# Layer norm of x applied to its transpose, and two bias adds issued as accumulating transfers

## The chip, the core and the metric

The kernel runs on one core of a Trainium2 chip. The core has TensorE (PE, matrix products; its weight loads are listed as PEld), VectorE (DVE), ScalarE (ACT), GpSimd (POOL) and SyncE (SP), which here only issues transfers; transfers run on 16 DMA engines. SP's transfers are in the queue q1, those that GpSimd issues in q0. The engines run their own instruction streams and wait for each other by semaphores. The metric is device time of one execution in microseconds (us), median of several runs.

## The reference

One transformer layer over 32 batches of 224 rows of width 512, all in 32-bit floats, three residual blocks one after another:

```python
x = x + attn(layernorm(x))                      # 16 heads of 32, softmax over 224 keys, output weight Wff, bias bff
x = x + xattn(ctx, ctx, layernorm(x))           # one head of 512, 750 keys from ctx (32, 750, 512), bias bo
x = x + ffn(layernorm(x))                       # per row: top 8 of 2048 keys, softmax, sum of 8 rows of a value table, a gate
def layernorm(x): m = mean(x); v = var(x); return (x - m) / sqrt(v + 1e-5)      # over the 512 columns
# attn: q = n @ Wq.T / sqrt(512); k = n @ Wk.T; v = n @ Wv.T, n = layernorm(x)
```

## The kernel before

**Stages.** Each batch of 224 rows is held as two tiles of 112 rows (`T, R = 2, 112`). The work of a batch is cut into steps of four stages: A is the self-attention, X the cross-attention, F the router (top 8 search), G the weighted sum of the looked-up value rows. One iteration of the main loop works on batch i in A, i-1 in X, i-2 in F and i-3 in G, so that the four stages of four batches overlap. Iterations 0 to 2 and the last are written out, 3 to B-2 are a hardware loop (`Fori`). What is left of X, F and G after the last iteration, and the scaling and adding of the looked-up sums to the output (step Z), follow in the table `LAST`.

**Order.** The table `ORDER` lists the steps of an iteration. Each engine has a function for its part of a step, and `pipeline` (L286 ff.) calls them on every engine in the table's order. So each engine's stream is fixed, and an engine that waits holds back all that stands behind the wait. `SETUP` puts the one-time weight products (W) between the steps of iteration 0.

**PSUM.** A has four banks, X and F two each. `FILLS` says how many fills a step makes; they go round the banks, and a fill waits until the one before it in its bank is drained (`wait_free`, `wait_full`, `wait_drained`). The number of A's fills in an iteration must be a multiple of 4.

**The steps of A.** For batch b: `norm` (DVE, `a_norm`, L742) makes mean and 1/deviation of each row of `xa` and overwrites `xa` with (x - m) * rstd. `turn` transposes it on PE, 8 products with the unit matrix into two fills; ACT casts each fill to a rounded high part `xT[0]` (`turn_hi`, L567), DVE subtracts to get the low part `xT[1]` (`turn_lo`, L775). `qk` k (k = 0 to 3, four heads each) makes queries and keys, 24 products of 224 columns (three per pair: high-high, high-low, low-high); ACT casts the result (`qk_hi`), DVE makes the low part (`qk_lo`). `value` makes two fills of 12 products with 512 columns; ACT copies them to `va`. `score` k multiplies, `maxima` (L794) and the exponentials (L586) follow, `share` (L805, L807) divides by the sum, `prob` transposes the shares on PE (L994) and ACT copies them to `paT`, `mix` multiplies by the values (L1072), ACT copies to `oT`.

**The steps of X and F named below.** X `enter` is the product with Wff, to which DVE adds x with its bias (`x_enter`, L819, tile `xr`, result `x1`); X `norm` normalises `x1`; X `out` t is added to `x1` and gives `x2` (L844), freeing the two banks that `enter` needs. F `norm` normalises `x2` and takes the variance of the result, F `top` is the search (L861, L864).

**GpSimd.** `bias_x` (L502) adds the bias bff to `xr` once a batch, `bias_x1` (L509) adds `cb` to `x1`, `add_base` (L514) adds the normalised x2 to x2. In between GpSimd issues the look-ups, two indirect transfers for each of 8 chunks of a batch (L523), which G sums up (L888, L890) on DVE.

**Start.** SP issues some 20 loads of weights and small vectors, then `xr`; `split_hi` and `split_lo` (L658 ff., L905 ff.) cut Wq, Wk and Wv into a high and a low part, straight from the loaded tiles.

```python
("A", "norm", 0), ("X", "enter", 0), ("A", "turn", 0), ("G", "sum", 0), ("X", "norm", 0), ("A", "qk", 0),
("A", "value", 0), ("X", "turn", 0), ("G", "sum", 1), ("A", "score", 0), ("G", "sum", 2), ("X", "query", 0),
("A", "share", 0), ("F", "norm", 0), ("A", "prob", 0), ("A", "qk", 1), ("A", "qk", 2), ("G", "sum", 3),
```

## Time and profile before

| | |
|---|---|
| median of three runs | 2863.55 us (2862.77 to 2865.97) |
| the profiled execution's own time | 2859.07 us |
| its span, first to last instruction | 2857.2 us |
| busy: PE, PEld | 2649.0 us (93%), 1983.5 us (69%) |
| busy: DVE, ACT, POOL | 2104.9 us (74%), 1421.1 us (50%), 785.7 us (27%) |
| share of the chain that ended last | PE 90%, issue 2%, DVE 2%, DMA 2%, ACT 1%, POOL 1% |
| transfers | 313.05 MB; q1 19.2% and q0 17.4% of the 16 engines' span |

A row of the chain or of a timeline begins with its start in us and its length; `L985` is a line of the kernel, `psA<-xT_hi,wqT_hi` the tile written and those read, `x48` the number of instructions. Successive matrix products overlap in their rows, so the pace is read from start to start. The hardware loop's iterations are alike; that of the rows below begins near 1587 us.

### The profile page before, as it was taken

The numbers are of one execution on the slowest core, as the hardware profiler recorded it, in microseconds if no ns is written. First come the engines' busy times: TensorE is split into PE (matmuls) and PEld (weight loads), VectorE is DVE, ScalarE is ACT, GpSimd is POOL, SyncE is SP. The second block draws the span as 40 slices with busy tenths as digits, with TensorE's granted clock in tenths as the row PEclk, the third lists the DMA queues.
The fourth block names the chain that finished last, engine by engine and source line by source line (L and its number), as shares of the span: only waits on it lengthen the run. The fifth ranks groups of instructions, "written<-read, shape, count | busy, mean of one in ns | idle before, by whom it ended". The sixth has DMA issues, their size and how long they took to land.

```text
span 2857.2 us, 53958 instructions
## 1 busy us (share of the span) xinstructions
PE 2649.0 (93%) x18042; PEld 1983.5 (69%) x18042; DVE 2104.9 (74%) x4071; ACT 1421.1 (50%) x4214; POOL 785.7 (27%) x651
## 2 busy tenths in 40 slices
PE   6899999999999999999999999999999999999830
PEld 4667777777777777777777777777777777777610
DVE  4446778878777788877777878777788877777652
ACT  2345554445455444555554445455544455555343
POOL 0001323222223232222323222223232222233245
PEclk9999999999999999999999999999999999999965
DMA  5112323333333332333323333333332333333799
GB/s 167 57 57 76 103 91 118 103 102 105 107 101 100 102 120 86 108 107 109 103 91 116 110 96 104 107 101 104 99 120 89 107 107 110 101 93 108 180 237 181
DMA packets 102683, 313.05 MB, mean 110 GB/s; under 512 B 14577, under 2 KB 15089, under 8 KB 94417
## 3 DMA queue, kind: packets, MB, share of 16 engines
q1 hardware_dynamic: 54002, 180.37, 19.2%
q0 software_dynamic: 48640, 132.16, 17.4%
q8 instruction: 23, 0.38, 0.1%
q14 instruction: 18, 0.15, 0.0%
HBM read 269.35 MB, written 43.12 MB: 109 GB/s over the span
## 4 chain that ended last, share of the span: by engine, by line
PE 90%; issue 2%; DVE 2%; DMA 2%; ACT 1%; POOL 1%; SPq 1%; POOLq 0%; DVEq 0%; ACTq 0%
PE psX L985 45%; PE psA L985 19%; PE psF L985 8%; PE psA L994 8%; PE psA L1072 4%; PE psA L1049 4%; PE psX L994 3%; DMA vg<-in_L_ffn_aux_values,idx 1%; DVE xT_lo L775 1%; PE psF L994 1%; ACT xT_hi L567 1%; POOL out L540 1%; POOL vg L523 0%; SPq L371 0%; ACT paT L550 0%
## 5 line engine op out<-in xcount | busy, mean ns | idle before, releaser
L523 POOL DMA_INDIRECT vg<-in_L_ffn_aux_values,idx x512 | 516.5, 1009 | 1635.1 <-DVE agg L890 830.9
L586 ACT ACTIVATE pa<-psA,nmax 112x224 f32<-112x224 f32 x1024 | 443.6, 449 | 150.3 <-DVE nmax L794 147.6
L890 DVE SCALAR_TENSOR_TENSOR agg<-vg,wt,agg 112x512 f32<-112x512 f32 x420 | 367.5, 875 | 16.2 <-DMA vg<-in_L_ffn_aux_values,idx 2.9
L794 DVE TENSOR_REDUCE nmax<-psA 112x4 f32<-112x896 f32 x256 | 266.7, 1083 | 149.8 <-PE psA L1049 149.8
L985 PE MATMUL psX<-big,gT 128*112 128x375 f32 x1024 | 333.4, 478 | 1.3 <-ACT nx L622 1.0
L985 PE MATMUL psX<-pT,cx 125*128 125x224 f32 x1536 | 307.5, 357 | 0.0
L550 ACT COPY paT<-psA 112x448 f32<-112x448 f32 x512 | 236.5, 544 | 111.1 <-PE psA L994 108.7
L985 PEld LDWEIGHTS psX<-pT,cx 125*128 125x128 f32 x1536 | 285.5, 190 | 7.7 <-issue 0.3
L807 DVE TENSOR_TENSOR pa<-pa,rsum 112x896 f32<-112x896 f32 x256 | 279.5, 1092 | 8.8
L985 PEld LDWEIGHTS psX<-big,gT 128*112 128x112 f32 x1024 | 177.4, 176 | 127.1 <-ACT nx L622 1.2
L985 PE MATMUL psX<-m,xnxT 128*112 128x512 f32 x512 | 235.6, 603 | 0.0
L994 PEld LDWEIGHTS psA<-ident,pa 112*112 112x112 f32 x2048 | 206.3, 136 | 42.3 <-issue 22.3
L994 PE MATMUL psA<-ident,pa 112*112 112x112 f32 x2048 | 227.6, 263 | 5.5 <-DVE pa L807 5.5
L985 PE MATMUL psX<-wffT,oT 128*112 128x512 f32 x512 | 225.0, 592 | 0.6 <-ACT oT L550 0.6
L586 ACT ACTIVATION_READ_ACCUMULATOR pa<-psA,nmax 112x1 f32 x1024 | 212.4, 207 | 0.0
L985 PE MATMUL psX<-xnxT,m 128*128 128x224 f32 x1024 | 204.5, 358 | 0.6 <-ACT xnxT L550 0.6
L572 ACT CAST qk_hi<-psA 128x448 fp32r<-128x448 f32 x128 | 68.2, 532 | 267.0 <-PE psA L985 267.0
L985 PE MATMUL psA<-xT_hi,wqT_hi 128*128 128x224 f32 x512 | 155.7, 304 | 46.9 <-DVE xT_lo L775 46.9
L985 PEld LDWEIGHTS psX<-xnxT,m 128*128 128x128 f32 x1024 | 192.9, 192 | 6.0 <-ACT xnxT L550 4.5
L985 PEld LDWEIGHTS psX<-wffT,oT 128*112 128x112 f32 x512 | 88.5, 177 | 131.7 <-issue 130.6
L861 DVE MAX8 top<-sc 112x8 f32<-112x2048 f32 x64 | 146.5, 2289 | 38.0 <-ACT sc L550 38.0
L622 ACT ACTIVATE nx<-psX,xmax 112x375 f32<-112x375 f32 x128 | 72.2, 569 | 203.4 <-DVE xmax L825 203.4
(195 smaller groups left out, 5301.5 us busy)
## 6 DMA issues: line engine op xcount, KB each, us to landing
big<-in_ctx_t SPq DMA_DIRECT2D x32, 1500.0 KB, 6.7
cx<-in_ctx SPq DMA_DIRECT2D x32, 1500.0 KB
xa<-in_x SPq DMA_DIRECT2D x32, 448.0 KB, 4.7
xr<-in_x SPq DMA_DIRECT2D x32, 448.0 KB, 3.9
out<-x SPq DMA_DIRECT2D x32, 448.0 KB, 3.1
agg_scratch<-agg SPq DMA_DIRECT2D x60, 224.0 KB, 6.4
vg<-in_L_ffn_aux_values,idx POOLq DMA_INDIRECT x512, 3.7
over_weights<-agg_scratch SPq DMA_DIRECT2D x15, 448.0 KB, 13.5
```

Of the source, the lines that this page charges most:

```text
L523: pool.indirect_dma_start(vg[:, c % SLOTS, k, :], None, aux_values, bass.IndirectOffsetOnAxis(ap=idx[:, t, n:n + 1], axis=0))\
L550: nc.scalar.copy(dst, src).then_inc(drained[s][j % banks[s]], 1)
L586: last = nc.scalar.activation(pa[:, t, h, :], psA[0:R, h, t * S:(t + 1) * S], ACT.Exp, bias=nmax[:, k % 2, h, t:t + 1], accum_out=rsum[:, ...
L622: nc.scalar.activation(px[:, t, j * HK:(j + 1) * HK], bank("X", job)[0:R, 0:HK], ACT.Exp, bias=xmax[:, t:t + 1], accum_out=xsum[:, t, j:j ...
L794: nc.vector.tensor_reduce(nmax[:, k % 2, h:h + 2, :], psA[0:R, h:h + 2, 0:T * S].rearrange("p h (t s) -> p h t s", t=T), AX_X, ALU.max, ne ...
L807: nc.vector.tensor_tensor(pa[:, t, :, :], pa[:, t, :, :], rsum[:, k, t, :].unsqueeze(2).to_broadcast([R, HB, S]), ALU.mult).then_inc(a_sha ...
L861: mark("F", nc.vector.max(top[:, t, :], sc[0:R, :]))
L890: last = nc.vector.scalar_tensor_tensor(dst, vg[:, c % SLOTS, k, :], w, dst, ALU.mult, ALU.add)
L985: last = nc.tensor.matmul(dst, stationary, moving, start=n == 0, stop=n == len(pairs) - 1)
L994: return nc.tensor.transpose(dst, src, ident[0:k, 0:k])
L1049: last = nc.tensor.matmul(psA[0:R, h, t * S:(t + 1) * S], qkT[q][own, k % 2, t * R:(t + 1) * R], qkT[key][own, k % 2, S:2 * S], start=n == ...
L1072: last = nc.tensor.matmul(bank("A", j)[h * DH:(h + 1) * DH, 0:S], va[:, c, HB * k + h, :], paT[:, c, h, :], start=c == 0, stop=c == T - 1)
```

## The change

**x turned outside.** A new input `x_t` holds x of each batch already transposed. SP loads it to `centered` (128 x 896). PE's `turn` of A is gone, and with it the normalisation of `xa`: DVE only takes the row statistics (stage N, for the batch after the one in A; 13 short steps). SP stores 1/deviation of the 224 rows to DRAM and loads them back spread over 128 partitions (`spread`). DVE multiplies `centered` by it, ACT casts to `xT[0]`, DVE subtracts for `xT[1]` (step N `center`).

**No mean in x.** The mean is taken out of the weights instead: at the start PE makes the column mean of Wq, Wk, Wv (a product with a matrix of 1/512), and DVE subtracts it from each before the split.

**value in quarters.** Four fills of 256 columns take the place of two of 512, so 48 products instead of 24; ACT copies four times.

**Biases.** `bias_x` and `bias_x1` are transfers that GpSimd issues with an accumulating add, 448 KB each, from the bias tile in SBUF.

**Order.** `ORDER` is a new table, `FIRST` stands before iteration 0, and the iteration before the last is written out too. `LAST` is unchanged.

```diff
-    ("A", "norm", 0), ("X", "enter", 0), ("A", "turn", 0), ("G", "sum", 0), ("X", "norm", 0), ("A", "qk", 0),
...
+    ("X", "enter", 0), ("X", "norm", 0), ("A", "qk", 0), ("G", "sum", 0), ("A", "value", 0), ("X", "turn", 0),
...
+    ("A", "prob", 3), ("F", "score", 3), ("A", "mix", 3), ("N", "center", 0), ("X", "out", 1), ("F", "top", 1),
-FILLS = {("A", "turn"): 2, ("A", "qk"): 1, ("A", "value"): 2, ("A", "score"): HB, ("A", "prob"): 2 * T,
+FILLS = {("A", "qk"): 1, ("A", "value"): 2 * T, ("A", "score"): HB, ("A", "prob"): 2 * T,
+FIRST = (("W", "mean", 0), ("N", "norm", 0), ("N", "spread", 0), ("W", "split", 0), ("W", "mean", 1), ("N", "center", 0),
+         ("W", "split", 1), ("W", "mean", 2), ("W", "split", 2),
+         ("W", "keys", 0), ("W", "keys", 1), ("W", "keys", 2), ("W", "keys", 3))
...
-                batch = {"A": i, "X": i - 1, "F": i - 2, "G": i - 3, "W": 0}
+                batch = {"N": i + 1, "A": i, "X": i - 1, "F": i - 2, "G": i - 3, "W": 0}
...
-            sp.dma_start(xa[:, :, :], tiles(row(x, 0))).then_inc(x_loaded, 16)
+            sp.dma_start(xa[:, :, :], pairs(row(x, 0))).then_inc(x_loaded, 16)
+            sp.dma_start(flat(centered), row(x_t, 0)).then_inc(xt_loaded, 16)
...
+            def store_moments(b, _):
+                sp.wait_ge(steps["N"], N_STEPS * (b + 1))
+                sp.dma_start(row(moments_dram, b), rstd["N"][:, :]).then_inc(moments_stored, 16)
+                if not (isinstance(b, int) and b == B - 1):
+                    sp.dma_start(xa[:, :, :], pairs(row(x, b + 1))).then_inc(x_loaded, 16)
+
+            def spread_moments(b, _):
+                sp.wait_ge(moments_stored, 16 * (b + 1))
+                wait(sp, xt_scaled, b)
+                sp.dma_start(spread[:, :], row(moments_dram, b).rearrange("r t -> (r t)").partition_broadcast(P))\
+                    .then_inc(moments_spread, 16)
+
+            def next_xt(b, _):
...
+                sp.wait_ge(xT_split, b + 1)
+                sp.dma_start(flat(centered), row(x_t, b + 1)).then_inc(xt_loaded, 16)
...
-                    nc.gpsimd.tensor_tensor(xr[:, :, :], xr[:, :, :], bff[:, :].unsqueeze(1).to_broadcast([R, T, D]),
-                                            ALU.add).then_inc(xr_biased, 1)
+                    apart(pool)
+                    pool.dma_start(xr[:, :, :], bff[:, :].unsqueeze(1).to_broadcast([R, T, D]), accum_op=ALU.add)\
+                        .then_inc(xr_biased, 16)
...
-                nc.gpsimd.tensor_tensor(x1[:, :, :], x1[:, :, :], cb[:, :].unsqueeze(1).to_broadcast([R, T, D]),
-                                        ALU.add).then_inc(x1_biased, 1)
+                apart(pool)
+                pool.dma_start(x1[:, :, :], cb[:, :].unsqueeze(1).to_broadcast([R, T, D]), accum_op=ALU.add)\
+                    .then_inc(x1_biased, 16)
...
+            def center_hi(b, _):
+
+                act.wait_ge(xt_scaled, b + 1)
+                wait_full(act, "A", max(FILL["A", "value", 0] + 2 * T - 1, FILL["A", "qk", NB - 1]), b - 1)
+                nc.scalar.copy(xT[0][:, :, :], centered[:, :, :]).then_inc(xT_hi, 1)
...
+            def scaled_x(b):
+                dve.wait_ge(xt_loaded, 16 * (b + 1))
+                dve.wait_ge(moments_spread, 16 * (b + 1))
+                nc.vector.tensor_tensor(centered[:, :, :], centered[:, :, :], spread[:, :].unsqueeze(1).to_broadcast([P, C, S]),
+                                        ALU.mult).then_inc(xt_scaled, 1)
+
+            def center_lo(b, _):
+                scaled_x(b)
+                dve.wait_ge(xT_hi, b + 1)
+                lo(xT[1][:, :, :], centered[:, :, :], xT[0][:, :, :]).then_inc(xT_split, 1)
...
+            def split_lo(_, n):
+                w = (wqT, wkT, wvT)[n]
+                nc.vector.tensor_tensor(staged[n], staged[n], made_next().unsqueeze(1).to_broadcast([P, C, D]), ALU.subtract)\
+                    .then_inc(setup_drained, 1)
...
-                    wait_drained(pe, "A", FILL["A", "turn", 0] + 1, b)
+                    pe.wait_ge(xT_split, b + 1)
...
+                for t in range(T):
+                    for half in range(2):
+                        j, cols = FILL["A", "value", 0] + 2 * t + half, slice(half * D // 2, (half + 1) * D // 2)
+                        wait_free(pe, "A", j, b)
...
+            def mean_weight(_, n):
+                if n == 0:
+                    pe.wait_ge(const_ready, 2)
+                pe.wait_ge(weight_loaded[n], 16)
+                product(place(), [(over_d, staged[n][:, c, :]) for c in range(C)]).then_inc(setup_full, 1)
```

`place()` waits until the setup product three before it is drained, so the fourth product of the router's keys (fill 6) waits for the third subtraction.

On PE, at the seam of the hardware loop and the first steps behind it, the kernel before (`wffT,oT` is X enter, `ident,xa` the transposes, `xT,wqT` the first of qk 0):

```order
L252 REGISTER_ALU
L985 MATMUL psX<-wffT,oT 112x512 x8
L1017 REGISTER_ALU
L252 REGISTER_ALU
L994 MATMUL psA<-ident,xa 128x112 x8
L252 REGISTER_ALU
L985 MATMUL psA<-xT_hi,wqT_hi 128x224
```

and the changed one:

```order
L257 REGISTER_ALU
L1041 MATMUL psX<-wffT,oT 112x512 x8
L1079 REGISTER_ALU
L257 REGISTER_ALU
L1041 MATMUL psA<-xT_hi,wqT_hi 128x224
```

The eight transposes are gone, and qk 0 follows X enter directly.

On DVE, at the start, the kernel before, behind the norm of batch 0 (`wqT_lo`, `wkT_lo`, `wvT_lo` are the split of the weights, `wffT<-psX` the router's keys):

```order
L738 TENSOR_SCALAR xa<-xa,mv_A,rstd_A 112x512 x2
L909 SCALAR_TENSOR_TENSOR wqT_lo<-cx,wqT_hi 128x512 x4
L909 SCALAR_TENSOR_TENSOR wkT_lo<-m,wkT_hi 128x512 x4
L909 SCALAR_TENSOR_TENSOR wvT_lo<-m,wvT_hi 128x512 x4
L913 COPY xnxT<-bvc 128x4x112
L775 TENSOR_TENSOR xT_lo<-psA,xT_hi 128x448 x2
L916 TENSOR_SCALAR wffT<-psX 112x512 x2
```

and the changed one, behind the statistics of batch 0 (`cx<-cx,psX` and `m<-m,psX` take the mean out of Wq and Wk, `m<-m,psF` out of Wv):

```order
L959 TENSOR_TENSOR cx<-cx,psX 128x2048
L964 SCALAR_TENSOR_TENSOR wqT_lo<-cx,wqT_hi 128x512
L964 SCALAR_TENSOR_TENSOR wqT_lo<-cx,wqT_hi 128x512 x3
L827 TENSOR_TENSOR centered<-centered,spread 128x896
L822 TENSOR_TENSOR xT_lo<-centered,xT_hi 128x896
L959 TENSOR_TENSOR m<-m,psX 128x2048
L964 SCALAR_TENSOR_TENSOR wkT_lo<-m,wkT_hi 128x512
L964 SCALAR_TENSOR_TENSOR wkT_lo<-m,wkT_hi 128x512 x3
L959 TENSOR_TENSOR m<-m,psF 128x2048
L964 SCALAR_TENSOR_TENSOR wvT_lo<-m,wvT_hi 128x512
```

The split of Wk and Wv now stands behind the multiplication by `spread`, which waits for the round through DRAM.

On DVE, at share 0 (`rsum` and `pa`), the kernel before (`stats_F` begins F norm):

```order
L883 ISA
L890 SCALAR_TENSOR_TENSOR agg<-vg,wt,agg 112x512
L709 REGISTER_ALU
L890 SCALAR_TENSOR_TENSOR agg<-vg,wt,agg 112x512
L805 RECIPROCAL rsum<-rsum 112x4
L709 REGISTER_ALU
L807 TENSOR_TENSOR pa<-pa,rsum 112x896
L805 RECIPROCAL rsum<-rsum 112x4
L709 REGISTER_ALU
L807 TENSOR_TENSOR pa<-pa,rsum 112x896
L252 REGISTER_ALU
L716 BN_STATS stats_F<-x 112x6 x2
```

and the changed one (`mv_F` and `var_all` are the end of F norm, `qk_lo` the low part of qk 1):

```order
L815 BN_AGGR mv_F<-stats_F 112x2 x2
L749 REGISTER_ALU
L818 ISA
L818 COPY var_all<-mv_F 112x2
L857 RECIPROCAL rsum<-rsum 112x4
L749 ISA
L859 TENSOR_TENSOR pa<-pa,rsum 112x896
L857 RECIPROCAL rsum<-rsum 112x4
L749 REGISTER_ALU
L859 TENSOR_TENSOR pa<-pa,rsum 112x896
L837 REGISTER_ALU
L822 TENSOR_TENSOR qk_lo<-psA,qk_hi 128x448
```

F norm now stands between the maxima of score 0 and share 0. On PE, prob 0 has moved from ahead of qk 1 and qk 2 to behind them and F turn.

## Rows read from the trace of the kernel before

**Rows 1.** Busy time by stretch: us, each engine's busy time (instructions), PEclk, DMA share, GB/s

```profile
357.00:2500.00 2143.00, 2105.88 (x14567) 1585.58 (x14566) 1693.49 (x3281) 1110.07 (x3354) 606.84 (x493) 1.00 0.33 104
```

**Rows 2.** The chain that ended last, whole run: start us, us, what

```profile
26.29 8.49 PE psA L985 x48
...
122.89 8.52 PE psA L985 x48
...
2588.16 8.52 PE psA L985 x48
```

**Rows 3.** The same chain, in one iteration

```profile
1587.26 10.48 PE psX L985 x24
1597.74 0.47 PE psA L994 x4
...
1598.24 0.54 ACT xT_hi L567
...
1599.34 0.62 DVE xT_lo L775
...
1600.01 8.52 PE psA L985 x48
...
1616.40 1.53 PE psA L994 x16
```

**Rows 4.** Waits: who for whom, us in total, times, longest

```profile
PE psA L985 <- DVE xT_lo L775: 46.9, 32, 2.7
```

**Rows 5.** Timeline of PE in that iteration: start us, us, instruction

```profile
1600.22 0.27 PE L985 MATMUL psA<-xT_lo,wqT_hi 128*128 128x224 f32 x1
...
1602.79 0.39 PE L985 MATMUL psA<-wvT_hi,xT_hi 128*112 128x512 f32 x1
...
1608.37 0.93 PE L994 MATMUL psX<-ident,nx 112*128 112x112 f32 x8
```

**Rows 6.** Timeline of DVE in that iteration

```profile
1601.72 1.28 DVE L716 BATCH_NORM_STATS2 stats_X<-x 112x6 f32<-112x512 f32 x2
...
1607.12 3.37 DVE L890 SCALAR_TENSOR_TENSOR agg<-vg,wt,agg 112x512 f32<-112x512 f32 x2
1610.40 2.08 DVE L794 TENSOR_REDUCE nmax<-psA 112x4 f32<-112x896 f32 x2
1612.40 1.53 DVE L890 SCALAR_TENSOR_TENSOR agg<-vg,wt,agg 112x512 f32<-112x512 f32 x2
...
1616.55 1.28 DVE L716 BATCH_NORM_STATS2 stats_F<-x 112x6 f32<-112x512 f32 x2
...
1623.86 1.14 DVE L775 TENSOR_TENSOR qk_lo<-psA,qk_hi 128x448 fp32r<-128x448 f32 x2
```

**Rows 7.** Timeline of POOL in that iteration

```profile
1606.74 2.40 POOL L509 TENSOR_TENSOR x<-x,cb 112x1024 f32<-112x1024 f32 x1 [1.96 <-DVE nx L738]
...
1621.52 2.38 POOL L514 TENSOR_TENSOR x<-x,nx 112x1024 f32<-112x1024 f32 x1 [4.09 <-DVE nx L738]
```

**Rows 8.** Transfers by line: number, KB each, median us from issue to landing

```profile
agg_scratch<-agg SPq DMA_DIRECT2D x60, 224.0 KB, 6.4
...
out<-over_weights POOLq DMA_DIRECT2D x15, 448.0 KB, 13.5
```

**Rows 9.** Timelines of PE and DVE at the start

```profile
18.01 3.72 PE L985 MATMUL psX<-sc,gT 128*112 128x512 f32 x4 [3.19 <-DMA unc1T<-in_L_ffn_unc_w]
...
52.31 2.28 DVE L775 TENSOR_TENSOR rkL<-wffT,rkS 49x2048 fp32r<-49x2048 f32 x1
```

**Rows 10.** The chain at the start

```profile
19.45 4.96 DMA gbc<-in_L_ffn_gate_bias
...
46.98 3.45 PE psX L985 x8
...
59.10 5.61 PE psA L985 x48
...
66.18 0.88 PE psA L1049 x23
```

More of the change, by code:

```diff
@@ L302, in iteration @@
                         step[s, name](b, arg)
+            for s, name, arg in FIRST:
+                if (s, name) in step:
+                    step[s, name](0, arg)
             for i in range(3):
                 iteration(i)
-            with eng.Fori(3, B - 1) as i:
+            with eng.Fori(3, B - 2) as i:
                 iteration(i)
+            iteration(B - 2)
             iteration(B - 1)
@@ L478, in _ @@
                           ("W", "cb"): first_cxT, ("W", "gb"): first_ctx,
-                          ("X", "score"): next_cxT, ("X", "mix"): next_ctx, ("A", "turn"): next_x, ("X", "enter"): next_xr,
+                          ("X", "score"): next_cxT, ("X", "mix"): next_ctx, ("N", "norm"): store_moments,
+                          ("N", "spread"): spread_moments, ("N", "center"): next_xt, ("X", "enter"): next_xr,
                           ("F", "norm"): store_base,
@@ L798, in share @@
             def share(b, k):
+                if k == 0:
+                    count["A"] = 0
                 for t in range(T):
@@ L971, in _ @@
                            ("W", "gb"): made_gb,
-                           ("A", "norm"): a_norm, ("A", "turn"): turn_lo, ("A", "qk"): qk,
+                           ("N", "norm"): x_moments, ("N", "center"): center_lo, ("A", "qk"): qk,
                            ("A", "score"): maxima, ("A", "share"): share,
@@ L1033, in value @@
                     pe.wait_ge(split, 3 * C)
-                wait_drained(pe, "A", FILL["A", "turn", 0] + 1, b)
+                pe.wait_ge(xT_split, b + 1)
                 for t in range(T):
-                    j = FILL["A", "value", 0] + t
-                    wait_free(pe, "A", j, b)
-                    filled("A", j, product3(bank("A", j)[0:R, :], [(both(xT, ALL, c, slice(t * R, (t + 1) * R)),
-                                                                    both(wvT, ALL, c, ALL)) for c in range(C)]))
+                    for half in range(2):
+                        j, cols = FILL["A", "value", 0] + 2 * t + half, slice(half * D // 2, (half + 1) * D // 2)
+                        wait_free(pe, "A", j, b)
+                        filled("A", j, product3(bank("A", j)[0:R, 0:D // 2],
+                                                [(both(xT, ALL, c, slice(t * R, (t + 1) * R)), both(wvT, ALL, c, cols))
+                                                 for c in range(C)]))
             def scores(b, k):
```

142 lines of the change are left out of this document (76 added, 66 removed), and 23 rows, old and new, of tables (ORDER, SETUP).

## The prediction

> **What bounds the kernel now.** I read the views in this order. The table of busy time by stretch shows the steady part: PE is busy 2105.88 of 2143 us, 98%, at the full clock (granted 1.00, so 2.4 GHz), DVE 79%, ACT 52%, the DMA engines 33% [rows 1]. So there a microsecond counts only if it is PE's. The chain of waits confirms it: it runs through PE, and one batch's qk 0 follows the last at a fixed distance. From the one at 1600.01 to that of batch 31 at 2588.16 are 12 batches, 82.35 us each [rows 2, 3]. Inside an iteration the chain leaves PE at one place only: after X enter come the transposes of `xa` at 1597.74, then ACT's cast, DVE's subtraction, and PE goes on at 1600.01, 2.27 us later [rows 3]. The list of waits has the same hole, 46.9 us in 32 waits, 1.47 us each [rows 4]; the rest of the 2.27 us is the transposes. Everything else in the iteration is PE work end to end.
>
> **Part 1, the transposes and their wait: -2.27 us a batch.** X enter is now followed by qk 0, which waits for `xT_split`. Is that in time? N center stands on DVE behind the last G sum and on ACT behind the copy of mix 3. From mix 3 on, PE has X out 1 and X enter to do, 10.48 us [rows 3]. In that time ACT must copy mix 3 (about 0.3) and cast 896 columns: 448 took 0.54, so 1.08 [rows 3]. DVE must subtract 896 columns: share 0, two reciprocals and two products of that size, takes 2.6 us in all (from the end of the 1.53 us sum at 1612.40 to F norm at 1616.55), so at most 1.3 [rows 6]. Together 2.7 us, and X out's second half, which DVE now takes behind it, is only full after 3.6 us. The 1/deviation is made early: N norm stands behind G sum 1, some 25 us after qk 0, and center at about 68. Within these 40 us lie a store and a load through DRAM; the nearest rows are 6.4 us for a store of 224 KB and 4.96 us for a small load in the crowded start [rows 8, 10]. So nothing is late next here.
>
> **Part 2, value in quarters: +0.43 us a batch.** The trace has no product of 256 columns of this kind. From 1600.22 to 1602.79 are 23 products of 224 columns, 0.1117 us each; from 1602.79 to 1608.37 24 of 512, 0.2325 us each [rows 5]. Between them a column costs 0.00042 us, so 256 columns cost 0.125 us and 48 products 6.01 us, against 5.58 now. Bounds: 48 times 0.1117 is 5.36 (a gain of 0.22), 48 times 0.2325 is 11.16 (a loss of 5.58). I take the line, since 224 columns lie next to 256 and have weight loads at least as wide (128 columns against 112).
>
> The Trainium skill (TensorE: Matmul & The Clock Gate, Back-to-back issue gap) says that the spacing of products is set by the weight load and the product together; the change doubles value's weight loads. Were the loads the bound, value would go to 11.16 us, and the whole to 2818 + 30 x 5.15 = 2972. The 0.1117 us of qk, with 24 loads of 128 columns, speaks against it: this trace has the load hidden. I give that under 1 in 100.
>
> **Part 3, the biases: 0 on PE.** GpSimd loses two adds of 2.4 us an iteration [rows 7] and gets two issues of 448 KB. No accumulating transfer into SBUF is in the trace. The nearest row, an accumulating transfer of 448 KB to DRAM in the crowded end, lands after 13.5 us [rows 8]; I take that as the upper bound and nothing as the lower. What covers it: `x1` is biased behind X norm and used in X out over 50 us later, `xr` at mix 0 and used in X enter 35 us later. Behind the bias of `x1` in GpSimd's queue stand the look-ups of chunk 2; they are summed in G sum 2, and between G sum 0 and G sum 2 DVE has maxima (2.0), F norm (7.3), share 0 (2.6) and more [rows 6], over 20 us. If the cover went, DVE would wait for the look-ups, and PE behind it.
>
> What goes besides is a stall of DVE: two sums of G took 3.37 us beside GpSimd's add to `x1`, two like them 1.53 us right after [rows 6, 7]. These 1.84 us are DVE's, in a stretch where PE does not wait for it, so they count nothing.
>
> The Trainium skill (SBUF — State Buffer, Who interferes with whom) has the rule for it: a DVE instruction with two SBUF inputs and a GpSimd instruction that reads SBUF exclude each other for a whole instruction. The trace agrees with the 3.37 against 1.53. The rule also speaks against the new order, see the first rival.
>
> **Part 4, the start: +9.5 us up to the second qk 0.** Before, the first qk 0 is at 26.29 [rows 2]. Now it waits for a round through DRAM. SP comes to the store of the deviations behind its twenty-odd loads: the last small one was issued at 19.45, `xr` comes 0.5 later, and the new load of `x_t` lies ahead of them (up to 1.6), so 22.0. The store lands as the small load did, 4.96 us later, 27.0; the load back, with little beside it, 4.0 later (my choice below those 4.96 us), 31.0 [rows 10]. Then multiply, cast, subtract: 1.2 + 1.1 + 1.2, 34.5. Only then does DVE come to Wk: a subtraction of 2048 elements, 2.28 us [rows 9], four casts (0.54 times 512/448, 0.62 each) and the last low part, 0.7: 40.0. Then the subtraction for Wv, 42.3, which the router's fourth key product waits for; two instructions at 0.93 us (four such took 3.72 when PE had just been idle [rows 9]): 44.2. So qk 0 comes 17.9 us late. Iteration 0 gives some back: before, PE was done with m2 at 50.43 and waited for share 0, and did qk 1 and qk 2 from 59.10 on, so that score 1 came at 66.18 [rows 10]. Now qk 1 and qk 2 stand in that wait, and score 1 follows prob 0 and its last copy, at 59.7: -6.5. With +0.4 for value and -2.3 for the transposes the second qk 0 moves from 122.89 by +9.5. Bounds: the round in half the time is 4.5 us less; both transfers as slow as 13.5 us is 18 more.
>
> **The sum.** +9.5 up to batch 1's qk 0, then 30 batches at -2.27 + 0.43 = -1.84 are -55.2, and value of batch 31 +0.4. The tail (`LAST`) is the same work. Together -45.3. The profiled execution took 2859.07 us (span 2857.2 and 1.9 around it), so 2813.8; the median of the runs lies 4.5 above that execution, so 2818.
>
> **Rivals.**
>
> First, slower: F norm now stands ahead of share 0, and prob 0 waits for share 0 and for the low parts of qk 1 and qk 2 (its last fill needs qk 2's bank). Counted from qk 0, DVE's maxima begin 2.03 us after X turn [rows 5, 6], which stands at 2.78 + 6.01 = 8.79: 10.8. With 2.0, F norm 7.3, share 0 2.6 and the two low parts 1.1, DVE is done at 23.9. PE reached prob 0 8.0 us after X turn [rows 3, 5]; with qk 1 and qk 2 (5.4) and F turn (0.9) it is there at 23.1, at its last fill at 24.2. The slack is 0.3 us. GpSimd's add of F starts when DVE's normalised x2 is there and runs 2.38 us [rows 7]; before, what came behind F norm at 1623.86 met its end at 1623.90. If the add comes late, because GpSimd is still issuing, it would hold share 0, which reads two SBUF tiles, for up to 2.38 us: 2.1 us a batch, 63 in all, 2881. It decides from a delay of 0.3 + 1.84 us. Against it: GpSimd has nothing to issue just then, G sum 0's look-ups being done about 5 us before.
>
> Second, a smaller gain: on ACT the two copies of F score 0 now stand directly ahead of the four of prob 2, and score 3 needs the banks that these free. Two copies of 512 columns are 1.2 us; if all of it falls on PE, 37 us, 2855, if half, 2837. For it: PE has only F score 1 between prob 2 and score 3, about 0.9 us. Against it: the copies of prob 2 are not longer than before, and ACT has been idle for part of F score 0's time.
>
> Third, the change does not do what it says: qk 0 waits for `xT_split` as it did for `xT_lo`, 1.47 us a batch, 2862. The slack worked out in part 1 speaks against it.
>
> **Numbers.** Forecast 0.70, its own range 2800 to 2836 (value between its lower bound and the line, the start between -5 and +18). Second rival 0.16, 2836 to 2862. Third 0.05. First 0.09, 2860 to 2881 and beyond. What a measurement of this kernel can tell from no change is about 0.2%, 5.7 us: faster is below 2857.8. That is the forecast and most of the second rival, 0.84; the third and the rest of the second, 0.06; slower 0.10. The range 2799 to 2855 leaves out the first and the third rival and the end of the second.
>
> **What would show it.** Right: 80.5 us from qk 0 to qk 0, 12 products of 256 columns in 1.50 us, no wait of PE between X enter and qk 0, the first qk 0 near 44 us and the second near 132. Wrong: a row in the list of waits of PE on `pa` or `qk_lo` of 30 or so times near 1 us (first rival), on `paT` (second) or on `xT_lo` (third); waits of DVE on the look-ups, which would mean that the accumulating transfers hold GpSimd's queue; a low granted clock in the steady part.

## The result, and the profile after

The changed kernel takes 2846.36 us (median of five runs, 2843.18 to 2849.35) against 2862.77 us of the kernel before, run on the same chip: 0.9941 of its time, 95% interval 0.9928 to 0.9953, so 16.4 us faster. The forecast was 2818. The profiled execution has a span of 2841.4 us where the kernel before had 2857.2: 15.8 us less, and these are accounted for below.

First the start. The chain of waits of the changed kernel, with the columns start, length, what:

```profile
21.43 6.17 DMA moments_scratch<-rstd_N
...
27.62 4.29 DMA spread<-moments_scratch
...
32.00 1.10 DVE centered L827
...
37.42 0.64 ACT wkT_hi L702
...
38.15 2.50 DVE wkT_lo L964 x4
...
42.90 2.05 PE psF L1041 x2
44.95 5.09 PE psA L1041 x36
...
132.23 8.23 PE psA L1041 x72
...
207.44 8.24 PE psA L1041 x72
287.34 8.23 PE psA L1041 x72
...
2571.39 8.23 PE psA L1041 x72
```

The round through DRAM, Wk behind it, the third subtraction and the router's last key product come one after the other as the prediction had them; the first qk 0 is at 44.95 us and the second at 132.23, 9.3 us later than before [rows 2]. From there to the qk 0 of batch 31 at 2571.39 are 30 batches and 2439.16 us; before they took 2465.27 [rows 2]. That is 26.1 us less, where the prediction has 55.2. The tail, 270.0 us against 269.0, adds 1.0. Together +9.3 - 26.1 + 1.0 = -15.8.

So the miss is in the 30 batches. The row 207.44 to 287.34 shows that not all of them are alike: iteration 2 takes 79.90 us, less than the 80.5 predicted. It has no batch in stage G yet, but that alone is not it: in the kernel before the same iteration takes 82.31 us (200.27 to 282.58), as much as those of its loop. From 287.34 on, 28 batches take 81.57 us each. The changed kernel's busy time over the stretch of [rows 1]:

```profile
357.00:2500.00 2143.00, 2105.62 (x15125) 1625.67 (x15124) 1677.70 (x3256) 1129.41 (x3394) 544.08 (x499) 1.00 0.47 123
```

PE is still at 98% and at the full clock. What is left of its waits, from 380 to 2570 us (engine, line, whom it waits for, us in total, times, longest):

```profile
PE psA L1130 <- ACT pa L626: 30.6, 27, 1.2
PE psA L1050 <- DVE qk_lo L822: 6.5, 25, 0.7
```

The wait for `xT_lo` [rows 4] is gone. Two others have come: mix 2 (L1130) waits for ACT's exponentials, 1.13 us in each of 27 batches, and prob 0 (L1050) for the low part of a qk, 0.26 us in each of 25 by this list. The list counts idle time only. By the starts, more is lost: X score, which follows prob 0, comes 0.4 us later after qk 0 in the iteration at 1591.86 than in iteration 2, and X out 0, which stands behind mix 2 and F score 2, 1.6 us later. Mix 2 puts its result into a bank that holds score 3 until the exponentials have read it. Here is the timeline of PE from the last products of score 3 to mix 2 and F score 2 (the idle time before an instruction and its releaser stand in brackets):

```profile
1647.83 0.30 PE L1107 MATMUL psA<-qk_hi,qk_lo 32*112 32x224 f32 x4
1648.06 4.81 PE L1041 MATMUL psX<-pT,cx 125*128 125x224 f32 x24
1654.01 0.96 PE L1130 MATMUL psA<-paT,va 112*32 112x224 f32 x16 [1.15 <-ACT pa L626]
1654.90 0.48 PE L1041 MATMUL psF<-rkS,rqS 112*112 112x512 f32 x1
```

DVE's maxima of score 3, ACT's last exponentials, and GpSimd's look-ups at the same time:

```profile
1649.49 2.09 DVE L844 TENSOR_REDUCE nmax<-psA 112x4 f32<-112x896 f32 x2 [2.08 <-PE psA L1107]
```

```profile
1650.62 0.45 ACT L626 ACTIVATE pa<-psA,nmax 112x224 f32<-112x224 f32 x1 [2.50 <-DVE nmax L844]
...
1653.74 0.46 ACT L626 ACTIVATE pa<-psA,nmax 112x224 f32<-112x224 f32 x1
```

```profile
1646.56 0.93 POOL L562 DMA_INDIRECT vg<-in_L_ffn_aux_values,idx  x1 [9.99 <-DVE agg L942]
1647.79 0.92 POOL L562 DMA_INDIRECT vg<-in_L_ffn_aux_values,idx  x1 [0.30 <-issue]
```

The same place in the kernel before, on PE and DVE:

```profile
1655.78 0.28 PE L1049 MATMUL psA<-qk_hi,qk_lo 32*112 32x224 f32 x4
...
1660.48 0.55 PE L985 MATMUL psF<-rkS,rqS 112*112 112x512 f32 x1
...
1661.65 0.96 PE L1072 MATMUL psA<-paT,va 112*32 112x224 f32 x16
```

```profile
1656.18 2.09 DVE L794 TENSOR_REDUCE nmax<-psA 112x4 f32<-112x896 f32 x2 [2.97 <-PE psA L1049]
```

Two things are to be seen. The row behind mix 2 is F score 2: in the kernel before it stood ahead of mix 2, and the new order has it behind, so only X mix 1 (4.81 us) lies between score 3 and mix 2. And the last product of score 3 ends at 1647.83 + 0.30 = 1648.13, but DVE, idle and waiting for PE, starts at 1649.49, 1.36 us later. Iteration 2, where GpSimd issues nothing between 228 and 271 us, has the same two instructions on PE and DVE like this:

```profile
263.03 0.29 PE L1107 MATMUL psA<-qk_hi,qk_lo 32*112 32x224 f32 x4
263.26 4.81 PE L1041 MATMUL psX<-pT,cx 125*128 125x224 f32 x24
267.99 0.96 PE L1130 MATMUL psA<-paT,va 112*32 112x224 f32 x16
```

```profile
263.43 2.09 DVE L844 TENSOR_REDUCE nmax<-psA 112x4 f32<-112x896 f32 x2 [3.63 <-PE psA L1107]
```

There DVE starts 0.11 us after the product's end, and mix 2 follows X mix 1 without a wait. The first profile of the kernel before has 0.12 at this place. The Trainium skill (TensorE: Matmul & The Clock Gate, The cost: per-tile semaphore tail) says that the semaphore increments of several tiles' products come one after another; for four tiles with four increments, as in a score, its formula gives 0.15 us, an estimate. The 0.11 us measured here lies near that, and the 1.36 us is not explained by it.

The same stands at score 0, whose end falls on the look-ups of G sum 0, here on PE, DVE and POOL:

```profile
1601.40 0.28 PE L1107 MATMUL psA<-qk_hi,qk_lo 32*112 32x224 f32 x4
...
1614.99 1.04 PE L1050 MATMUL psA<-ident,pa 112*112 112x112 f32 x8 [0.16 <-DVE qk_lo L822]
```

```profile
1602.50 2.09 DVE L844 TENSOR_REDUCE nmax<-psA 112x4 f32<-112x896 f32 x2 [2.32 <-PE psA L1107]
```

```profile
1601.04 1.01 POOL L562 DMA_INDIRECT vg<-in_L_ffn_aux_values,idx  x1 [1.45 <-DVE agg L942]
```

The maxima start 0.82 us after the product's end (1601.68), where iteration 2 has 0.11, and F norm, share 0 and the low parts of qk 1 and qk 2, which stand behind them on DVE, come that much later for prob 0.

### The profile page after: what moved, and what is told of

The parts are those of the page before. It is cut to its first block, busy times and chain, and to the rows that moved or that the text cites. A ratio compares the mean times of both kernels' runs of the same rounds, so it can differ in the third digit from the quotient of the medians.

```text
span 2841.4 us, 55248 instructions
## 1 busy us (share of the span) xinstructions
PE 2633.9 (93%) x18578; PEld 2016.2 (71%) x18578; DVE 2075.9 (73%) x4010; ACT 1436.4 (51%) x4246; POOL 702.9 (25%) x652
## 4 chain that ended last, share of the span: by engine, by line
PE 74%; DVE 10%; issue 8%; ACT 3%; DMA 2%; POOL 1%; SPq 1%; DVEq 1%; POOLq 0%; ACTq 0%
PE psX L1041 34%; PE psA L1041 13%; PE psF L1041 9%; PE psA L1050 6%; PE psA L1107 6%; PE psA L1130 4%; PE psX L1050 2%; ACT pa L626 2%; DVE nmax L844 2%; DMA vg<-in_L_ffn_aux_values,idx 1%; DVE stats_F L757 1%; DVE nx L784 1%; DVE stats_F L810 1%; DVE qk_lo L822 1%; POOL out L579 1%
## 5 line engine op out<-in xcount | busy, mean ns | idle before, releaser
L562 POOL DMA_INDIRECT vg<-in_L_ffn_aux_values,idx x512 | 507.6, 991 | 1247.2 <-DVE agg L942 660.3
L942 DVE SCALAR_TENSOR_TENSOR agg<-vg,wt,agg 112x512 f32<-112x512 f32 x420 | 314.7, 749 | 14.9 <-DMA vg<-in_L_ffn_aux_values,idx 1.6
L589 ACT COPY paT<-psA 112x448 f32<-112x448 f32 x512 | 242.9, 547 | 91.9 <-PE psA L1050 90.0
L1050 PE MATMUL psA<-ident,pa 112*112 112x112 f32 x2048 | 228.0, 262 | 8.8 <-DVE qk_lo L822 8.0
L1050 PEld LDWEIGHTS psA<-ident,pa 112*112 112x112 f32 x2048 | 205.2, 134 | 41.4 <-issue 19.6
L548 POOL DMA_DIRECT2D x<-cb x32 | 38.9, 1217 | 636.5 <-DVE nx L784 636.5
L1041 PEld LDWEIGHTS psX<-m,xnxT 128*112 128x112 f32 x512 | 87.8, 176 | 112.5 <-issue 108.5
## 6 DMA issues: line engine op xcount, KB each, us to landing
xr<-bff POOLq DMA_DIRECT2D x32, 448.0 KB, 10.7
```

The costliest lines, as they stand in the source:

```text
L562: pool.indirect_dma_start(vg[:, c % SLOTS, k, :], None, aux_values, bass.IndirectOffsetOnAxis(ap=idx[:, t, n:n + 1], axis=0))\
L589: nc.scalar.copy(dst, src).then_inc(drained[s][j % banks[s]], 1)
L942: last = nc.vector.scalar_tensor_tensor(dst, vg[:, c % SLOTS, k, :], w, dst, ALU.mult, ALU.add)
L1041: last = nc.tensor.matmul(dst, stationary, moving, start=n == 0, stop=n == len(pairs) - 1)
L1050: return nc.tensor.transpose(dst, src, ident[0:k, 0:k])
```

## Experiments

Theory: the loss against the forecast is 1.2 us a batch at mix 2 and 0.5 at prob 0. Each needs two things: an order that leaves no cover (F score 2 behind mix 2; F norm ahead of share 0), and a late release of scores 3 and 0, where GpSimd's look-ups fall on the end of the score. Rivals: the cover alone does it; the accumulating transfers do it; the late release is the kernel's own, of the change. Ratios are to the kernel before on the same chip, with 95% intervals.

### F score 2 ahead of mix 2 again

```diff
-    ("X", "mix", 1), ("A", "share", 3), ("A", "mix", 2), ("F", "score", 2), ("X", "out", 0), ("G", "sum", 7),
+    ("X", "mix", 1), ("A", "share", 3), ("F", "score", 2), ("A", "mix", 2), ("X", "out", 0), ("G", "sum", 7),
```

> The changed kernel with one step moved: F score 2 stands ahead of A mix 2 again, as before the change. In the changed kernel mix 2 waits 1.14 us in nearly every iteration (27 waits, 30.6 us between 380 and 2570) for ACT's exponentials of score 3, with nothing but X mix 1 between score 3 and it. Theory 1 (the order lost a cover): F score 2 takes 1.11 us of PE and stands in the hole, the wait falls to under 0.1 us, the distance from qk 0 to qk 0 goes from 81.5 to 80.4 us, and the time to about 2846 - 28 x 1.1 = 2815. Rival (the hole is not there but moves): F score 2's copies wait on ACT for the search of F top 0 and hold mix 2's copy, something behind it waits as long, and the time stays within 6 us of 2846.

2825.64 us, 0.9874 (0.9858 to 0.9891): 20.7 us less than the changed kernel. Its waits of PE over the same stretch:

```profile
PE psA L1050 <- DVE qk_lo L822: 8.0, 25, 0.7
PE psA L1130 <- ACT pa L626: 4.9, 25, 0.2
```

The cover takes 1.13 us a batch down to 0.2. Score 3 is still released late: its last product ends at 1637.70, and DVE's maxima start only at 1639.03. So the order of F score 2 carries the largest part of the miss. It came out 10 us above the 2815 expected: most iterations take 80.62 us, a quarter of them 81.2.

### Both sums moved off the ends of scores 0 and 3

```diff
-    ("X", "enter", 0), ("X", "norm", 0), ("A", "qk", 0), ("G", "sum", 0), ("A", "value", 0), ("X", "turn", 0),
+    ("X", "enter", 0), ("X", "norm", 0), ("A", "qk", 0), ("A", "value", 0), ("X", "turn", 0),
...
-    ("G", "sum", 1), ("N", "norm", 0), ("F", "turn", 0),
+    ("G", "sum", 0), ("G", "sum", 1), ("N", "norm", 0), ("F", "turn", 0),
...
-    ("A", "mix", 1), ("A", "share", 2), ("F", "score", 0), ("A", "prob", 2), ("F", "score", 1), ("G", "sum", 5),
+    ("A", "mix", 1), ("G", "sum", 5), ("A", "share", 2), ("F", "score", 0), ("A", "prob", 2), ("F", "score", 1),
```

> The changed kernel with two steps of G moved: sum 0 goes from behind qk 0 to just ahead of sum 1, and sum 5 goes ahead of A share 2, so that the look-ups which GpSimd issues behind them no longer fall on the ends of scores 0 and 3. In the changed kernel PE's release of score 3 to DVE comes 1.2 to 1.3 us late and that of score 0 0.7 to 1.4 us late in every iteration from the fourth on, where an issue of look-ups lies on it; scores 1 and 2, and iterations 0 to 2, which have no look-ups there, are released within 0.1 us. Theory 2 (the releases are late because look-ups are issued at that moment): DVE's maxima start 0.1 us after each score, the wait of mix 2 (1.14 us) and of prob 0 (0.25) go, the period is 80.1 us, and the time about 2846 - 28 x 1.4 = 2807. Rival (the lateness belongs to scores 0 and 3 themselves): maxima start as late as now, period 81.5, time within 6 us of 2846.

2989.75 us, 1.0458 (1.0437 to 1.0480). Scores 0 and 3 are now followed by their maxima within 0.13 us, as expected. Of score 1, on which look-ups now fall, the run says nothing: its maxima start 1.8 us after its end, but DVE is busy with the statistics of N and X's maximum until 0.13 us before. The time was lost elsewhere. DVE at sum 4, and PE at prob 1:

```profile
1628.04 0.49 DVE L940 TENSOR_SCALAR agg<-vg,wt 112x512 f32<-112x512 f32 x1 [3.47 <-DMA vg<-in_L_ffn_aux_values,idx]
```

```profile
1629.90 0.99 PE L1050 MATMUL psA<-ident,pa 112*112 112x112 f32 x4 [2.90 <-DVE qk_lo L822]
```

Sums 0, 1, 2, 3 and 4 stand so close that sum 4 waits for the data of its look-ups; behind it on DVE stands the low part of qk 3, and PE waits for that. The table by stretch, with the columns of [rows 1], shows what comes after:

```profile
1625.00:1630.00 5.00, 2.10 (x21) 1.89 (x21) 1.93 (x4) 2.60 (x8) 0.85 (x1) 0.91 0.96 335
1630.00:1635.00 5.00, 5.00 (x40) 4.57 (x41) 1.51 (x4) 0.97 (x2) 1.97 (x2) 0.50 0.89 219
```

After the wait the granted clock is 0.50, 1.2 GHz, in a stretch in which PE is busy all the time. So the run answers for the releases of scores 0 and 3; for the time it answers nothing.

### The adds on GpSimd back

```diff
-                    apart(pool)
-                    pool.dma_start(xr[:, :, :], bff[:, :].unsqueeze(1).to_broadcast([R, T, D]), accum_op=ALU.add)\
-                        .then_inc(xr_biased, 16)
+                    nc.gpsimd.tensor_tensor(xr[:, :, :], xr[:, :, :], bff[:, :].unsqueeze(1).to_broadcast([R, T, D]),
+                                            ALU.add).then_inc(xr_biased, 1)
```

(`bias_x1` likewise.)

> The changed kernel with its third part undone: the biases are added to x and x1 by GpSimd's additions (2.4 us each), the rest as it is. Theory 2a (it is the accumulating transfers on GpSimd's queue that make the releases late): the releases of scores 0 and 3 come within 0.2 us again, the wait of mix 2 goes, period about 80.4 us, time about 2815. Theory 2b (issuing look-ups on the end of a score is enough): score 3 is still released 1.2 us late, mix 2 waits 1.1 us, and the time stays within 8 us of 2846.

2850.73 us, 0.9962 (0.9947 to 0.9976). Without the transfers score 0 is released on time and score 3 is still late:

```profile
1652.62 0.30 PE L1105 MATMUL psA<-qk_hi,qk_lo 32*112 32x224 f32 x4
...
1658.58 0.96 PE L1128 MATMUL psA<-paT,va 112*32 112x224 f32 x16 [0.93 <-ACT pa L624]
```

```profile
1654.06 2.09 DVE L842 TENSOR_REDUCE nmax<-psA 112x4 f32<-112x896 f32 x2 [1.31 <-PE psA L1105]
```

From 1652.92 to 1654.06 are 1.14 us, and mix 2 waits 0.93. The accumulating transfers are not the cause of the wait at mix 2. They are worth at most a few us in this order: the intervals of the two kernels overlap. Prob 0 no longer waits in the loop, in line with the theory, but the last part of prob 1 now does, for the low part of qk 3 (11.9 us in 26 waits).

Iteration 2 of this run, 81.79 us where the changed kernel has 79.90, shows what the transfers take away. GpSimd's add to `xr` falls on the first product of share 0:

```profile
228.60 3.15 DVE L857 TENSOR_TENSOR pa<-pa,rsum 112x896 f32<-112x896 f32 x1
```

```profile
228.42 2.38 POOL L539 TENSOR_TENSOR xr<-xr,bff 112x1024 f32<-112x1024 f32 x1
```

The product takes 3.15 us instead of 1.09, and prob 0 waits for it. That is what the prediction's first rival feared of another add, and near its price of 2.1 us.

### The transfers alone, in the kernel before

```diff
-                    nc.gpsimd.tensor_tensor(xr[:, :, :], xr[:, :, :], bff[:, :].unsqueeze(1).to_broadcast([R, T, D]),
-                                            ALU.add).then_inc(xr_biased, 1)
+                    apart(pool)
+                    pool.dma_start(xr[:, :, :], bff[:, :].unsqueeze(1).to_broadcast([R, T, D]), accum_op=ALU.add)\
+                        .then_inc(xr_biased, 16)
```

(`bias_x1` likewise.)

> The kernel before with the third part alone: x and x1 get their biases by accumulating transfers, all else as before. My prediction put this part at 0 us. Theory 2a: releases of PE that meet an issue of look-ups come late here too, by 0.5 us or more, where before the change none of some 700 did; the time need not move, since those places have slack: within 10 us of 2863. Theory 2b: all releases stay within 0.1 us, and the time is 2863, within 6 us.

2871.23 us, 1.0031 (1.0020 to 1.0041): the transfers alone make the kernel before some 9 us slower. Its score 0 ends at 1617.40 + 0.28 = 1617.68, and the maxima follow 0.83 us later, beside a look-up that GpSimd issues at 1617.06:

```profile
1618.51 2.09 DVE L796 TENSOR_REDUCE nmax<-psA 112x4 f32<-112x896 f32 x2 [2.30 <-PE psA L1051]
```

```profile
1617.06 1.01 POOL L525 DMA_INDIRECT vg<-in_L_ffn_aux_values,idx  x1 [0.92 <-DVE agg L892]
```

Sum 0, which releases that look-up, shows how it came there:

```profile
1614.68 1.53 DVE L892 SCALAR_TENSOR_TENSOR agg<-vg,wt,agg 112x512 f32<-112x512 f32 x2
```

Before, it took 3.37 us beside GpSimd's add [rows 6, 7] and ended behind score 0 (1610.11 by PE's timeline), so that its look-ups were issued only at 1611.31. Now DVE's stall is gone, as predicted, and the 1.84 us that it gives back bring the look-up forward on the end of score 0. Most iterations go from 82.35 to 82.6 us, some to 82.9 or 83.2; the average from the fourth qk 0 on is 82.70, which makes 9.9 us over 28 batches. PE loses most of it at prob 0: in an iteration of 82.6 us its second half, which needs share 0, starts 17.2 us after qk 0 instead of 17.0. So a late score 0 costs PE time here too, with share 0 still ahead of F norm. The profile's later second qk 0 (124.24) and longer tail (271.4 us) say nothing: two other profiles of the kernel before, below, have a tail of 271.3 us and, with only F score 2 moved, a second qk 0 at 124.33.

### The kernel before, profiled once more

No edit.

> The kernel before, unchanged, profiled once more beside the others. In the first profile none of its releases by PE came over 0.12 us late, also those that end within an issue of look-ups; in the changed kernel and in the two variants e3 and e4 such releases came 0.25 to 1.5 us late. Theory 2b (it depends on where a look-up's issue stands to the end of the product, and before had no score there): the releases are on time again in this profile, as in the first, qk 0 to qk 0 82.35 us. Rival (the lateness belongs to the chip or the day, not to the kernel): this profile shows late releases as well, mix releases 0.3 us after the start of an issue among them.

2862.64 us, period 82.37. In the loop of the first profile no release of an idle DVE or ACT by PE came later than 0.14 us. In this one score 1, shortly after an issue of look-ups, is followed by its maxima 0.22 to 0.32 us after its end instead of 0.16, once 0.87, and ACT's copies of prob start 0.4 to 0.9 us late 50 times; PE waits for nothing but `xT_lo` all the same. So theory 2b missed, and its rival is right that late releases are not bound to the change: the kernel before has them too, fewer of them, differing from one execution to another, and with enough slack they cost nothing.

### Sum 5 alone ahead of share 2

```diff
-    ("A", "mix", 1), ("A", "share", 2), ("F", "score", 0), ("A", "prob", 2), ("F", "score", 1), ("G", "sum", 5),
+    ("A", "mix", 1), ("G", "sum", 5), ("A", "share", 2), ("F", "score", 0), ("A", "prob", 2), ("F", "score", 1),
```

> The changed kernel with G sum 5 alone moved, from behind F score 1 to ahead of A share 2, so that the look-ups issued behind it (at 1646.56 in the changed kernel) come some 4 us sooner and are over when score 3 ends. F score 2 stays behind mix 2. The data that sum 5 needs has landed at about 1640.4, when DVE would come to it. Theory 2: score 3 is released within 0.1 us, its exponentials end 1.25 us sooner, mix 2's wait of 1.14 us is under 0.1 us without any cover, period 80.4, time about 2815. Rival (the release of score 3 is late for another reason, or the exponentials end too late anyhow): the wait of mix 2 stays near 1.1 us, time 2846.

2837.86 us, 0.9909 (0.9893 to 0.9926). PE and DVE at score 3:

```profile
1645.00 0.36 PE L1107 MATMUL psA<-qk_hi 32*112 32x224 f32 x4 [0.86 <-ACT paT L589]
...
1645.58 0.29 PE L1107 MATMUL psA<-qk_hi,qk_lo 32*112 32x224 f32 x4
1645.81 4.81 PE L1041 MATMUL psX<-pT,cx 125*128 125x224 f32 x24
1650.55 0.96 PE L1130 MATMUL psA<-paT,va 112*32 112x224 f32 x16
```

```profile
1645.98 2.09 DVE L844 TENSOR_REDUCE nmax<-psA 112x4 f32<-112x896 f32 x2 [2.75 <-PE psA L1107]
```

With the look-ups moved to 1639 us, score 3 is released 0.11 us after its end, and mix 2 does not wait, though F score 2 still stands behind it. So the cover alone does not make the wait: the late release is needed too. In its place score 3 waits for ACT's copies of prob 2, 22.7 us in 30 waits, since share 2 is now behind sum 5 on DVE. That is the place of the prediction's second rival, brought about by this edit.

### F score 2 behind mix 2, in the kernel before

```diff
-    ("F", "top", 0), ("F", "score", 2), ("A", "share", 3), ("A", "mix", 2), ("X", "out", 0), ("G", "sum", 7),
+    ("F", "top", 0), ("A", "share", 3), ("A", "mix", 2), ("F", "score", 2), ("X", "out", 0), ("G", "sum", 7),
```

> The kernel before with one order move of the change alone: F score 2 goes behind mix 2, as in the changed kernel. Here no look-ups are issued between 1643.8 and 1663.8 in the iteration whose score 3 ends at 1656.1, so score 3 is released on time. Theory (the loss at mix 2 needs both, a late release of score 3 and the missing cover): DVE's maxima start at 1656.2, the eight exponentials end about 4.5 us later, at 1660.7, X mix 1 ends at 1660.8, so mix 2 waits 0.2 us or less, period 82.3 to 82.6, time within 6 us of 2862. Rival (the missing cover alone costs 1.1 us): PE waits 0.9 to 1.2 us for the exponentials at mix 2 in every iteration, period 83.4, time about 2894.

2863.27 us, 1.0005 (0.9996 to 1.0015). No look-up is near score 3 in this order, the maxima start at 1658.54, 0.13 us after the product's end at 1658.41, and mix 2 goes on without a wait:

```profile
1658.34 4.81 PE L985 MATMUL psX<-pT,cx 125*128 125x224 f32 x24
1663.08 0.96 PE L1072 MATMUL psA<-paT,va 112*32 112x224 f32 x16
```

This is the other half of the test: the same loss of cover, without the look-ups, costs nothing.

### Sum 0 at the head of the iteration

```diff
-    ("X", "enter", 0), ("X", "norm", 0), ("A", "qk", 0), ("G", "sum", 0), ("A", "value", 0), ("X", "turn", 0),
+    ("G", "sum", 0), ("X", "enter", 0), ("X", "norm", 0), ("A", "qk", 0), ("A", "value", 0), ("X", "turn", 0),
```

> The changed kernel with G sum 0 alone moved, from behind qk 0 to the head of the iteration, ahead of X enter, so that the look-ups issued behind it are over some 20 us before score 0 ends. Theory 2: score 0 is released within 0.1 us in every iteration (now 0.7 to 1.5 us late), DVE's maxima, F norm and share 0 come 0.75 to 1.3 us sooner, and PE's wait for the low parts of qk 1 and qk 2 at prob 0's last fill (25 waits, 6.5 us between 380 and 2570) and its second half's wait for share 0 go, as do the iterations that are 0.6 us longer than the rest. Mix 2's wait of 1.14 us stays, since score 3 is not touched. Period 81.5 less 0.3 to 0.5, time 2846 - 30 x 0.4 = 2834. Rival (prob 0 does not wait because of the late release, F norm ahead of share 0 is long enough by itself): period 81.5, time 2846.

2850.79 us, 0.9962 (0.9950 to 0.9975), where 2834 was expected. Score 0 ends at 1608.26 and the maxima start on time; prob 0 no longer waits. But PE has a new wait at value, whose last quarter needs the bank of qk 0, and the low part of qk 0 now stands behind sum 0 and the rest on DVE:

```profile
1605.02 0.37 PE L1041 MATMUL psA<-wvT_hi,xT_hi 128*112 128x256 f32 x1 [0.49 <-DVE qk_lo L822]
```

```profile
1608.38 2.09 DVE L844 TENSOR_REDUCE nmax<-psA 112x4 f32<-112x896 f32 x2 [3.41 <-PE psA L1107]
```

11.7 us in 25 waits, X turn is later by 0.75, and the iterations take 81.85 us. Prob 0's wait goes with the late release, as in the run with the adds back; the remedy costs more than it brings.

### center of batch 0 behind the weights' splits

```diff
-FIRST = (... ("W", "mean", 1), ("N", "center", 0),
-         ("W", "split", 1), ("W", "mean", 2), ("W", "split", 2),
+FIRST = (... ("W", "mean", 1),
+         ("W", "split", 1), ("W", "mean", 2), ("W", "split", 2), ("N", "center", 0),
```

> The changed kernel with one step of the start moved: N center of batch 0 stands behind the splits of Wk and Wv instead of ahead of them, so that DVE and ACT do these while the 1/deviation is on its way through DRAM (DVE waits 12.9 us for it now). The prediction charged the start 9.5 us up to the second qk 0, 9 of which are the splits queued behind center. If that step was right: the first qk 0 comes at 35.5 us instead of 44.0, the second 6 to 9 us sooner than 131.7, the time is about 2838. Rival (iteration 0 waits for something else anyway, the loads of the other weights): the first qk 0 is sooner, the second is not, time 2846.

2844.51 us, 0.9937 (0.9918 to 0.9956). The first qk 0 comes at 35.46 us, as expected, and the second 7.3 us earlier than in the changed kernel. In time only 2 us are left. Of the iterations from the third on, nine take 82.1 us and four 81.8 here, where three of the changed kernel take 82.1; nearly all others take 81.5. From the third qk 0 to batch 31's they take 2369.35 us against 2363.95, so 5.4 us of the start's gain are given back. In the nine, as in the three of the changed kernel, score 0's maxima start some 1.4 us after the product's end instead of 0.8. Why these are more here is open.

### The edits together

F score 2 ahead of mix 2 and center of batch 0 last:

```diff
-    ("A", "share", 3), ("A", "mix", 2), ("F", "score", 2),
+    ("A", "share", 3), ("F", "score", 2), ("A", "mix", 2),
-    ("W", "mean", 1), ("N", "center", 0), ("W", "split", 1), ("W", "mean", 2), ("W", "split", 2),
+    ("W", "mean", 1), ("W", "split", 1), ("W", "mean", 2), ("W", "split", 2), ("N", "center", 0),
```

> The changed kernel with both repairs that stand alone so far: F score 2 ahead of mix 2 (e1, measured 2826) and N center of batch 0 behind the splits (e7). If the two are independent the gains add: 2826 less what e7 brings, about 2818. If the start's gain is given back later, 2826.

F score 2 ahead of mix 2 and sum 0 at the head:

```diff
-    ("X", "enter", 0), ("X", "norm", 0), ("A", "qk", 0), ("G", "sum", 0),
+    ("G", "sum", 0), ("X", "enter", 0), ("X", "norm", 0), ("A", "qk", 0),
-    ("A", "share", 3), ("A", "mix", 2), ("F", "score", 2),
+    ("A", "share", 3), ("F", "score", 2), ("A", "mix", 2),
```

> F score 2 ahead of mix 2 (e1) and G sum 0 at the head (e9) together. Both waits of PE are then off: period 80.6 - 0.4 = 80.2 us, which is what the prediction's terms give without a loss in value's quarters (82.35 - 2.27 + 0 = 80.1), time about 2826 - 12 = 2814. Rival: the gains overlap (prob 0's wait is only passed on to mix 2), 2822 or more.

All three:

```diff
-    ("X", "enter", 0), ("X", "norm", 0), ("A", "qk", 0), ("G", "sum", 0),
+    ("G", "sum", 0), ("X", "enter", 0), ("X", "norm", 0), ("A", "qk", 0),
-    ("A", "share", 3), ("A", "mix", 2), ("F", "score", 2),
+    ("A", "share", 3), ("F", "score", 2), ("A", "mix", 2),
-    ("W", "mean", 1), ("N", "center", 0), ("W", "split", 1), ("W", "mean", 2), ("W", "split", 2),
+    ("W", "mean", 1), ("W", "split", 1), ("W", "mean", 2), ("W", "split", 2), ("N", "center", 0),
```

> All three: F score 2 ahead of mix 2, G sum 0 at the head, N center of batch 0 behind the splits. With e7 and e8 the start's 7 us were won up to the second qk 0 and lost again in iterations that were 0.6 us longer, which came oftener there; these iterations are those in which the release of score 0's first heads falls behind the second look-up's issue instead of ahead of it. With sum 0 at the head there are none: 2814 - 6 = 2808. Rival (the start's gain is given back by something else): 2814.

2830.78 us (0.9884, 0.9868 to 0.9901), 2831.11 (0.9888, 0.9872 to 0.9905) and 2826.01 (0.9868, 0.9852 to 0.9885). All three missed by 13 to 18 us: the gains of the single edits do not add up. Most iterations take 81.1 to 81.5 us, and the lists of PE's waits from 380 to 2570 us say where. With center last and F score 2 ahead, prob 0 waits 15.4 us in 25 waits, more than twice the changed kernel's. With sum 0 at the head, value waits for the low part of qk 0, 11.7 us in 26 waits (14.3 with all three), and mix 2 still 8.3 us in 26 (7.5). The one edit of F score 2 (2825.64) and all three together are the best versions, not to be told apart, some 36 us below the kernel before.

## Why the prediction was right in sign and too large in size

**The transposes and their wait.** Right. X enter is followed by qk 0 at once, and the third rival is out: no wait for `xT_split` is in the list.

**value in quarters.** Predicted +0.43 us a batch, and it costs nothing. From 1594.37 to 1599.93 are 48 products of 256 columns:

```profile
1594.37 0.28 PE L1041 MATMUL psA<-wvT_hi,xT_hi 128*112 128x256 f32 x1
...
1599.93 0.93 PE L1050 MATMUL psX<-ident,nx 112*128 112x112 f32 x8
```

That is 5.56 us, 0.116 each, against 5.58 in halves; the first 12 took 1.36 us (to 1595.73), where 1.50 was forecast. The line between 224 and 512 columns gave 0.125; the value lies closer to the 224 columns than to the line. The doubled weight loads did not show.

**The biases.** In the changed kernel right: the transfer to `xr` lands after 10.7 us (at most 13.5 predicted) and is covered. As a rule wrong: alone, in the kernel before, the transfers cost some 9 us (1.0020 to 1.0041). The 1.84 us of DVE that they free were put down as counting nothing; they do count, since GpSimd's look-ups follow DVE's sum and come earlier with it.

**The start.** Right: 44.95 for 44.2, and +9.3 for +9.5.

**The step that failed is the sum.** "Then 30 batches at -2.27 + 0.43 = -1.84" takes it that PE gets no new wait; the term for one is nothing. The work alone did better than that, 79.90 us in iteration 2, 0.6 below the 80.5. From iteration 3 on, two waits took 1.7 us back: about 1.2 at mix 2 and 0.5 at prob 0, 28 times, some 47 us; less the 30 times 0.6 us that the work does better, 29 us are missing, as the accounts at the top have it (55.2 against 26.1). Of mix 2 the prediction says nothing. Its second rival looks at ACT's copies ahead of score 3, one step earlier, and that wait is not in the changed kernel's list; that the time landed in this rival's range, and inside the whole range of 2799 to 2855, is luck. What I passed over is in the tables: F score 2 moved from ahead of mix 2 to behind it, some 1.1 us of PE's work that was the cover between score 3 and the bank that mix 2 needs. With F score 2 put back, 20.7 us return; with the look-ups moved away, the wait goes as well; with F score 2 moved in the kernel before, nothing happens. So the wait at mix 2 has two conditions, and both are shown.

**The first rival** had the right place, prob 0 behind share 0, and the slack of 0.3 us. Its cause, an add of GpSimd that is held back by issuing, was not it: in the iteration at 1591.86 the add starts at 1609.48, 0.1 us after DVE's normalised x2. The maxima of score 0 start 0.8 us late, which is above the slack, so part of the rival came true: 0.5 us a batch in place of 2.1. The add is on this path all the same. DVE's small copy ahead of share 0 ends 0.03 us after it in all 32 batches, in both kernels, and mostly takes 0.63 us, where the copy to `gate` of the same shape takes 0.16. So share 0 begins when the add ends, and the add begins when the late maxima let it.

**What stays open.** Why a product's end is told to DVE up to 1.5 us late when GpSimd issues an indirect transfer around that time, and why the first profile of the kernel before shows none of it. The runs show only where it occurs. For prob 0 only the late release was tested: no run put share 0 ahead of F norm again in the changed kernel, so that part of the theory is argued. Also open is whether an order that combines the edits reaches the 80.2 us.

## What to carry to other kernels

When an order is rewritten, list for each result bank which work stands between its last reader and its next writer, before and after, on the engine that bounds the kernel; a cover of 1 us that leaves costs that much as soon as the reader is 1 us late. A slack below some 1.5 us behind a product's end should not be counted on if GpSimd issues look-ups at the time. When several small shifts are each worth a us or less, run them together before adding up their gains.
